# Moving the maximum of x, the normalising and the opening's order in a one-core attention and FP4 feed-forward kernel

## What is computed

```python
def fp4_quant_dequant(x):
    scale = max(max(abs(block)) / 6.0, 1e-12)
    idx = searchsorted(_MID, abs(block / scale))
    return _GRID[idx] * sign(block) * scale

x = x + attention(layernorm(x), ctx)
xn = layernorm(x)
h = silu(fp4_linear(xn, w_gate)) * fp4_linear(xn, w_up)   # 256 -> 704
x = x + fp4_linear(h, w_down)                             # 704 -> 256
```

## Time and profile before

| | |
|---|---|
| runs | 468.27, 468.79, 470.64 us (median 468.79) |
| the profiled execution | 469.22 us, of which span 467.4 us |
| busy in the span | PE 443.4 (95%), PEld 296.6, DVE 431.9 (92%), ACT 408.8 (87%), POOL 251.1 (54%) |
| granted TensorE clock, mean | 0.989 |
| chain that ended last | PE 40%, DVE 33%, issue 12%, DMA 6%, ACT 5% |

### The profile page before, as it was taken

The page is one execution under the profiler, slowest core; times in us unless marked ns, Lnnn a source line. Parts: engine busy times, 40 slices in busy tenths (PEclk is TensorE's granted clock), DMA queues, the critical chain, the costliest instruction groups (busy, mean ns, idle before and its releaser), DMA issues.

```text
span 467.4 us, 10007 instructions
## 1 busy us (share of the span) xinstructions
PE 443.4 (95%) x3388; PEld 296.6 (63%) x3388; DVE 431.9 (92%) x766; ACT 408.8 (87%) x710; POOL 251.1 (54%) x346
## 2 busy tenths in 40 slices
PE   4999998888699999999999999999999999999996
PEld 4987887734256666666666666666666666666675
DVE  3699979759999999999999999999999999999893
ACT  3369979779989999999999999999999999987694
POOL 4056872555566555566655566666666665433330
PEclk9999999999889999999999999999999999999999
DMA  7999911342267666666666666676656676655562
GB/s 242 338 349 350 356 34 35 80 111 60 64 120 127 141 140 141 139 137 131 131 130 131 137 139 147 133 141 131 142 131 139 140 124 135 120 114 122 121 136 78
DMA packets 162003, 67.95 MB, mean 145 GB/s; under 512 B 126368, under 2 KB 161696, under 8 KB 161952
## 3 DMA queue, kind: packets, MB, share of 16 engines
q1 hardware_dynamic: 161952, 67.31, 61.9%
HBM read 27.38 MB, written 9.18 MB: 78 GB/s over the span
## 4 chain that ended last, share of the span: by engine, by line
PE 40%; DVE 33%; issue 12%; DMA 6%; ACT 5%; SPq 2%; POOL 1%; DVEq 0%; ACTq 0%; POOLq 0%
PE ps L1056 7%; PE ps L1058 7%; PE ps L1057 7%; PE ps L1084 7%; DVE hb L1362 6%; DVE y_h L1473 6%; DVE bm L1479 4%; PE ps L1087 4%; DVE ctx_sb L1367 3%; DVE bm L1503 2%; PE ps L908 2%; PE ps L885 2%; DVE bm L1498 2%; PE ps L895 2%; DMA xs<-in_x_dram 2%
## 5 line engine op out<-in xcount | busy, mean ns | idle before, releaser
L1056 PE MATMUL ps<-guT_hi,a_xT 128*128 128x512 f16 (+1 forms) x384 | 140.5, 366 | 9.0 <-DVE hb L1362 5.5
L1057 PE MATMUL ps<-guT_lo,a_xT 128*128 128x512 f16 (+1 forms) x384 | 140.5, 366 | 0.0
L1058 PE MATMUL ps<-guT_hi,a_xT 128*128 128x512 f16 (+1 forms) x384 | 140.4, 366 | 0.0
L1084 PE MATMUL ps<-dT_hi,hqT 128*128 128x256 f16 x704 | 124.5, 273 | 0.9 <-ACT hqT L728 0.5
L545 POOL TENSOR_TENSOR ctx_sb<-w_q_lo,sl 128x704 f16<-128x704 f16 x60 | 90.1, 1520 | 4.1 <-DVE ctx_sb L1430 4.1
L1087 PE MATMUL ps<-dT_lo,hqT 128*128 128x256 f16 x384 | 87.4, 273 | 0.0
L1084 PEld LDWEIGHTS ps<-dT_hi,hqT 128*128 128x128 f16 x704 | 68.9, 98 | 11.0 <-issue 0.9
L561 POOL TENSOR_TENSOR sl<-bm,sh 128x240 f16<-128x240 f32 (+2 forms) x33 | 31.3, 949 | 78.4 <-DVE y_h L1473 73.9
L703 ACT ACTIVATE w_raw<-ps,inv_gu 128x704 f32<-128x704 f32 x64 | 53.8, 840 | 18.7 <-PE ps L1058 18.5
L628 POOL TENSOR_TENSOR xs<-xs,w_raw 128x512 f32<-128x512 f32 x30 | 36.9, 1229 | 61.8 <-DVE ctx_sb L1367 58.6
L1056 PEld LDWEIGHTS ps<-guT_hi,a_xT 128*128 128x128 f16 x384 | 38.0, 99 | 44.9 <-DMA a_xT<-ctx_sb 8.4
(11 more groups left out here) (189 smaller groups left out, 807.5 us busy)
## 6 DMA issues: line engine op xcount, KB each, us to landing
xs<-in_x_dram SPq DMA_DIRECT2D x16, 512.0 KB, 8.7
ctx_sb<-in_ctx_dram SPq DMA_DIRECT2D x16, 512.0 KB, 8.2
out_dram<-a_xT SPq DMA_DIRECT2D x64, 128.0 KB, 2.1
w_raw<-a_scratch SPq DMA_DIRECT2D x60, 128.5 KB, 2.7
hqT<-ctx_sb SPq DMA_TRANSPOSE x62, 3.8
w_raw<-in_L_ffn_w_down_dram SPq DMA_DIRECT2D x1, 704.0 KB, 8.0
w_raw<-in_L_ffn_w_gate_dram SPq DMA_DIRECT2D x1, 640.0 KB, 5.2
w_raw<-in_L_ffn_w_up_dram SPq DMA_DIRECT2D x1, 640.0 KB, 6.3
```

Of the source, the lines that this page charges most:

```text
L1056: pe.matmul(dst, xt[:, c, :], guT[0][:, c, n0:n1], start=(c == 0), stop=False)
L1057: pe.matmul(dst, xt[:, c, :], guT[1][:, c, n0:n1], start=False, stop=False)
L1058: last = pe.matmul(dst, xt[:, KC + c, :], guT[0][:, c, n0:n1], start=False, stop=(c == KC - 1))
L1084: last = pe.matmul(dst, hqT[:, j % 4, c, :], dT_hi[:, c, :], start=(c == 0 and not preset(j)), stop=(c == DCH - 1))
```

## The change

In a steady step two calls move: VectorE takes `largest_x(st + 3)` directly behind `inverses(st)`, ahead of `products_x`, and ScalarE calls `normalise_x(st + 3)` ahead of `silu(2 * st)` from step 2 on. The opening's loops are written out: ScalarE takes Silu(0) ahead of the normalising of pair 2 and Silu(1) ahead of that of pair 3, and the copies of weights later; POOL takes its additions ahead of the statistics and behind other events; VectorE takes the first two `gate_up` between parts of x(1) and x(2). TensorE gets fillers after pair 0 (7), before pair 2 (5) and after it (12), and its last weight transposes move from pair 1 to pair 2. In the drain `turn_last(0)` goes ahead of `down(61)` and `turn_last(1)` directly behind it, and ScalarE's last residual goes behind the first two copies of transposed h. The diff, cut (POOL's, ScalarE's and VectorE's functions that are called keep their bodies; `stats` and `attend` are POOL's two blocks made into functions):

```diff
@@ POOL
+            stats(1)
+            low_scales_first(1)
+            pool.wait_ge(s["x1_done"], 2)
+            pool.wait_ge(s["x4_steps"], K_XQ)
+            attend(2)
+            pool.wait_ge(s["yx_done"], 2)
+            attend(3)
+            low_scales(-1)
+            stats(2)
+            pool.wait_ge(s["x4_steps"], 2 * K_XQ)
+            attend(4)
+            stats(3)
+            low_scales(0)
+            pool.wait_ge(s["h_steps"], 2)
+            attend(5)
+            for st in range(1, END):
...
-                    elif st == 1:
-                        pool.wait_ge(s["x4_steps"], K_XQ * (st + 1) + 2)
                     else:
-                        need(pool, s["yx_done"], n - 2)
+                        pool.wait_ge(s["yx_done"], 4)
+                    attend(st + 5)
@@ ScalarE
             split_first(1)
-            for st in range(-2, END):
+            normalise_x(1)
+            evacuate_weights(act, range(GU_FILLS, GU_FILLS + 1))
+            square_x(2)
+            scale_high(-1)
+            split_x(1)
+            silu(0)
+            normalise_x(2)
+            square_x(3)
+            silu(1)
+            scale_high(0)
+            split_x(2)
+            normalise_x(3)
+            square_x(4)
+            for st in range(1, END):
                 j, n = st - 1, st + 2
-                if st < 0:
-                    if st == -1:
-                        scale_high(st)
-                        split_x(n)
-                    normalise_x(st + 3)
-                    square_x(st + 4)
-                    if st == -2:
-                        evacuate_weights(act, range(GU_FILLS, GU_FILLS + 1))
-                elif st == 0:
-                    silu(0)
-                    normalise_x(st + 3)
-                    square_x(st + 4)
-                    scale_high(st)
-                    silu(1)
-                    split_x(n)
-                    evacuate_weights(act, range(GU_FILLS + 1, GU_FILLS + 2))
-                elif st < NP:
+                if st < NP:
                     residuals(2 * st - 8)
                     square_x(st + 4)
                     scale_high(st)
                     residuals(2 * st - 7)
+                    if st >= 2:
+                        normalise_x(st + 3)
                     silu(2 * st)
                     preset_x(2 * st - 6)
-                    if st == 1:
-                        evacuate_weights(act, range(GU_FILLS + 2, GU_FILLS + 3))
-                    if st == 2:
-                        evacuate_weights(act, range(GU_FILLS + 4, len(FILLS)))
-                    normalise_x(st + 3)
+                    if st <= 2:
+                        evacuate_weights(act, range(GU_FILLS + 2 * st - 1, GU_FILLS + 2 * st))
+                    if st < 2:
+                        normalise_x(st + 3)
                     if st == NP - 1:
                         split_h(j)
                         preset_x(2 * st - 5)
                     silu(2 * st + 1)
+                    if st == 2:
+                        evacuate_weights(act, range(GU_FILLS + 4, len(FILLS)))
                     if st < NP - 1:
                         preset_x(2 * st - 5)
                         split_h(j)
                     split_x(n)
                     if st == 1:
-                        evacuate_weights(act, range(GU_FILLS + 3, GU_FILLS + 4))
+                        evacuate_weights(act, range(GU_FILLS + 2, GU_FILLS + 3))
...
                     residual(2 * NP - 4)
-                    residual(2 * NP - 3)
                     keep_turned(0)
                     keep_turned(1)
+                    residual(2 * NP - 3)
                     keep_turned(2)
                     keep_turned(4)
@@ TensorE
-                if final:
-                    if j % 2 == 0:
-                        out_ready(pe, 2 * NP - 5)
-                        turn_last(0)
-                elif preset(j):
+                if preset(j):
...
-                        if c:
-                            turn_last(1)
...
+                if n == NP + 2:
+                    out_ready(pe, 2 * NP - 5)
+                    turn_last(0)
                 if tile_ok(2 * n - 7):
                     down(2 * n - 7)
+                if n == NP + 2:
+                    turn_last(1)
                 if n == NP:
                     open_down(2 * NP - 4)
                 if pair_ok(n):
+                    if n == 2:
+                        pe.wait_ge(s["w_ev"], GU_FILLS + 2)
+                        filler(5, 7)
                     gate_and_up(2 * n)
-                    if n == 1:
+                    if n == 2:
                         transpose_weights(GU_FILLS + 3)
                     gate_and_up(2 * n + 1)
-                if n < 2:
-                    transpose_weights(GU_FILLS + 2 + 2 * n)
+                if n == 0:
+                    pe.wait_ge(s["w_ev"], GU_FILLS + 1)
+                    filler(7, 6)
+                    transpose_weights(GU_FILLS + 2)
+                if n == 2:
+                    pe.wait_ge(s["w_ev"], GU_FILLS + 3)
+                    filler(12, 6)
+                    transpose_weights(GU_FILLS + 4)
@@ VectorE
-            for st in range(-1, END):
+            scales(-1)
+            inverses(-1)
+            dve.wait_ge(sc, 2 * (-1 - SC0) + 2)
+            scaling_x(1)
+            offset_x(1)
+            grid_x(1)
+            products_x(1)
+            gate_up(0)
+            largest_x(2)
+            scales(0)
+            inverses(0)
+            dve.wait_ge(sc, 2 * (0 - SC0) + 2)
+            scaling_x(2)
+            gate_up(1)
+            largest_h(0)
+            offset_x(2)
+            grid_x(2)
+            products_x(2)
+            largest_x(3)
+            scales(1)
+            inverses(1)
+            dve.wait_ge(sc, 2 * (1 - SC0) + 2)
+            scaling_h(0)
+            scaling_x(3)
+            largest_x(4)
+            for st in range(2, END):
                 j, p, xa, xb = st - 1, st - 2, st + 1, st + 2
-                if st == 0:
-                    offset_x(xa)
-                    grid_x(xa)
-                    products_x(xa)
-                    largest_x(xb)
                 if pair_ok(j) and st < NP:
                     gate_up(2 * j)
-                    if st == 1:
-                        largest_x(3)
                     gate_up(2 * j + 1)
                     largest_h(j)
                 if st < NP:
@@ -1582,16 +1616,17 @@
                     scales(st)
                     if pair_ok(p):
                         grid_h(p)
-                    if st >= 1 and pair_ok(xa):
+                    if pair_ok(xa):
                         offset_x(xa)
                     if pair_ok(p) and st < NP - 1:
                         high_h(p)
-                    if st >= 1 and pair_ok(xa):
+                    if pair_ok(xa):
                         grid_x(xa)
                     if tile_ok(2 * st - 7) and added(2 * st - 7):
                         residual(2 * st - 7)
                     inverses(st)
-                    if st >= 1 and pair_ok(xa):
+                    largest_x(st + 3)
+                    if pair_ok(xa):
                         products_x(xa)
                     if scaled(st):
                         dve.wait_ge(sc, 2 * (st - SC0) + 2)
@@ -1602,8 +1637,6 @@
                         turned_product(p, 0, 1).then_inc(s["z_lo"], 1)
                     if pair_ok(xb):
                         scaling_x(xb)
-                    if st >= 1:
-                        largest_x(st + 3)
```

More of the change, by code:

```diff
@@ L585, in _, with stats, attend @@
             low_scales_first(0)
-            for st in range(-3, END):
+            def stats(n):
+                pool.wait_ge(s["sq_done"], n + 1)
+                need(pool, s["xn_ready"], n - 1)
+                pool.tensor_scalar(s_ve[:, n % 2], s_sq[:, n % 2], 1.0 / D, LN_EPS, ALU.mult, ALU.add).then_inc(s["pool_st"], 1)
+                pool.wait_ge(s["pool_st"], K_R * n + 1)
+                pool.tensor_tensor(s_r[:, n % 2], s_ve[:, n % 2], neg_half[:, 0:2], ALU.pow).then_inc(s["pool_st"], 1)
+                pool.wait_ge(s["pool_st"], K_R * n + 2)
+                pool.tensor_tensor(s_nmr[:, n % 2], s_nm[:, n % 2], s_r[:, n % 2], ALU.mult).then_inc(s["pool_st"], 1)
+            def attend(n):
+                pool.wait_ge(attn_loaded[n % 2], 32 * (n // 2))
+                need(pool, s["pool_st"], K_R * (n - 1))
+                x1 = xs[:, 2 * n:2 * n + 2, :]
+                pool.tensor_tensor(x1, x1, attn[:, n % 2, :, 0:D], ALU.add)
+                pool.tensor_tensor(s_nm[:, n % 2], neg_mean[:, 2 * n:2 * n + 2], attn[:, n % 2, :, D], ALU.add
+                                   ).then_inc(s["x1_done"], 1)
+            stats(1)
[14 more added lines that the diff above has]
+            for st in range(1, END):
                 if st == NP:
@@ L598, in _ @@
                         last_low_scales(t)
-                if st == -1:
[L600 to L609, removed]
```

(31 more changed lines are left out.)

1 line of the change is left out of this document (removed).

## The result

The changed kernel takes **476.7 us** (median of 8 runs, 475.89 to 478.94) against 468.87 (8 runs, 468.27 to 470.64) of the kernel before: ratio 1.0172, 95% interval 1.0152 to 1.0192. It is slower by 1.7%, as forecast (475.2, range 471 to 478).

The account below looks back on a forecast made before the run. It took the loop from one y_h to the next (VectorE, ScalarE's split and residual, TensorE) as the bound; 469.22 + 8.0 steady - 0.8 opening - 0.75 drain = 475.7, less 0.4: 475.2 us, range 471 to 478.

Parts of the forecast that it names:

- The steady steps: Steps 5 to 27: odd steps lengthen by 0.49 us and even ones by 0.18, +8.0 us over 12 pairs.
- Both covers: Steady steps: VectorE would wait for ScalarE's normalising in odd steps (+0.49 us) and for the split of h in even (+0.18).
- The opening: Before the steady steps: -0.3 us from the new order and -0.5 from the clock, sum -0.8.
- 12 pairs of steps: Steady stretch: the moves' cost was counted over odd steps 5 to 27, +0.67 us per pair, +8.0 us.
- My walk: Opening: followed the earlier gate_up(1) through pair 2, fillers and copies to the split of h(1); gain -0.3 us.
- The clock's -0.5: Opening: with fillers in TensorE's 3.74 us gap, full clock ends pair 3 earlier and removes a 0.50 us VectorE wait.
- upper bound of +2.5: Opening: the loss if the clock falls again in spite of the fillers, +2.5 us.
- The drain: Last pair: transposes ahead of down(61) remove TensorE's 0.55 us idle and half a residual; -0.75 us, between 0 and -1.0.
- The lock decides: Rival, steady steps: normalising and split are ready, the lock's 0.24 us per odd step is gained; 465.1 us, chance 0.09.
- Only the split is late: Rival, steady steps: only the split's wait costs, +0.12 us a pair, +1.4, cancelled by opening and drain; 468.7, chance 0.07.
- The clock falls: Rival, opening: TensorE drops to the lower clock again after a stall before pair 4; +2.5 us, 477.7, chance 0.08.
- The signs: Expected in the profile: odd-step normalising wait 0.5 to 0.7 us, even-step split wait 0.1 to 0.2, TensorE's wait about 0.4.

Follow-up runs that it names:

- E3: The kernel before with only VectorE's maximum of x moved behind the reciprocals, from step 2 on; ScalarE's order unchanged: 507.32 us, ratio 1.0823.
- E6: The changed kernel with the normalising also put ahead of ScalarE's second residual: 473.59 us, ratio 1.0088.
- E11: The changed kernel with the maximum of x behind the reciprocals in even steps only, back behind the scalings in odd ones: 470.22 us, ratio 1.0027.
- E12: The changed kernel with POOL's second low-half product of a step over half its columns from pair 4 on: 477.71 us, ratio 1.0195.
- E4: The kernel before with only ScalarE's normalising moved ahead of the first Silu, from step 2 on: 468.71 us, ratio 0.9996.
- E9: The kernel before with the drain's change alone: 467.99 us, ratio 0.9987.
- E2: The changed kernel with the two steady moves undone, keeping the new opening, fillers and drain: 466.65 us, ratio 0.9956.
- E10: E2 without its three fillers: 466.52 us, ratio 0.996.
- E1: The kernel before with only the two steady-step moves, from step 2 on; opening and drain as before: 478.19 us, ratio 1.0204.
- E5: The changed kernel with VectorE's small `scales` put ahead of the offset of h: 478.25 us, ratio 1.0177.
- E7: The changed kernel with both `scales` ahead of the offset and the normalising ahead of ScalarE's second residual: 474.31 us.
- E8: The kernel before with POOL's two low products of h put behind its statistics, beside VectorE's two-input operations: 488.45 us, measured once.

## Why the prediction was right, point by point

**The steady steps: right in mechanism, 0.8 small in size.** Both covers went, one by one as worked out. Odd steps came to 11.59 for 11.53, even ones to 11.38 for 11.36; the odd step's excess is in the two products behind the maximum, 225.99 - 225.32 = 0.67 instead of the 0.61 of the earlier trace rows, because the first no longer takes 0.36. Over twelve pairs the forecast was 8.0, measured 8.82. That the normalising sets the odd step is shown by E3 (1.1 us later, 1.1 us longer) and E6 (0.36 earlier, 0.36 shorter); that the split sets the even one by E11 and E12.

**The opening: the net near, its terms off, and that they cancelled is luck.** gate_up(1) came 3.14 us earlier (forecast 3.46), y_h of pair 0 and TensorE's pair 2 2.5 earlier (2.9). I forecast -0.8 for the whole and the profiled stretch to E of pair 3 gave -0.49, but as the difference of two larger terms. With the old steps that stretch takes 53.05, 51.94 and 52.51 with the old order (before, E4, E9; mean 52.5) and 50.85 and 50.59 with the new one (E2, E10; 50.7): the order is worth **-1.8**. With the changed steps it takes 53.63 with the old order (E1) and 51.79 to 52.56 with the new one (the changed kernel, E5, E6, E7, E12; mean 52.2): the steady moves cost **+1.1 to +1.5** here already, since they begin in step 2 (the maximum waits 0.44 at 121.01). The step that failed is "12 pairs of steps" from step 5 on: I costed the moves only where the step has its final form.

My walk gave the order -0.3. It was right in kind: the splits of h(0) and h(1), which start 0.04 behind y_h with the old order, start 1.1 and 0.9 to 1.9 behind it in all kernels with the new one, and that is where the gain goes. But with the old steps it took back too much (E2, E10). The clock's -0.5 rests on one execution: the 0.50 that VectorE waits at 139.75 stands in the trace of the kernel before, where the clock is 0.50 in 125 to 130 and the step takes 11.78; E9, with the same opening and the same gap of 3.74 us, has 0.71 there, no such wait and 11.19. With runs of one order 1.1 apart, no term here is better known than by some 0.5. One slip beside: the opening's upper bound of +2.5 put in for -0.8 gives 478.5, not the 477.5 of my numbers.

**The drain: right** where nothing hides it: -0.85 in E9's stage, -0.75 forecast. In the changed kernel's own profiled execution one slow DMA covered it.

**The sum.** E1's +9.5 and E2's -2.1 make 7.4; measured 7.8.

**The rivals.** *The lock decides* fell because the normalising is ready at E + 8.66, not + 8.0; E8 shows that the lock is no fiction. By the exclusive lock of the Trainium skill's page "SBUF — State Buffer" (who interferes with whom) alone the change should gain; E8 agrees with its rule, 1.67 against 0.88, and the order of the kernel decided otherwise. *Only the split is late* fell with the waits for L743. *The clock falls* did not happen: it is 1.00 in every 5 us from 110 to 150. The Trainium skill's page "TensorE: Matmul & The Clock Gate" (HAM oscillation) has the clock go back in waits between bursts. E10 agrees, with 2.40 us of idle time ahead of pair 2 and 0.73 behind it, and shows no price in its median.

**The signs.** L1519 waits 0.46 in every odd step (forecast 0.5 to 0.7); the even step's wait is 0.17 (0.1 to 0.2), seen as 1.71 for 1.54, since the table of waits does not list it; TensorE's wait at the opening matmul grew from 3.7 to 7.1 in 100 us, by 0.4 a step to 0.8; my "grown to about 0.4 a step" fits the growth only, since 3.7 in nine steps was 0.4 already; the 0.60 of the product is gone.

**The better version.** E2, and E10 with it, beats both kernels, the kernel before by 0.4%: 466.65 and 466.52 against its 468.7 and 468.4 beside them. Keep opening and drain, leave the steady steps as they were.

## What to carry to other kernels

An operation that seems to stand in the wrong place may be the cover of a wait on either side of it: before moving it, work out when its own input is ready, and what the next operation in its old slot would then wait for. When VectorE and ScalarE feed each other in a loop, 0.25 us saved on one is lost if the hand-over then comes 0.7 us early for the other. And a move made in every step has its price from the first step on that has it: count it in the opening too.

## What the runs showed of the hardware that I had not expected

- **POOL's smallest operations stretch most.** In the changed kernel the three statistics of 128x2 took 0.86, 1.42 and 0.56 us (231.76 to 234.76) beside VectorE's 16-bit operations with two SBUF inputs. In E8, where they fall beside VectorE's `gate_up`, which has one of its inputs in PSUM, they take 0.19, 0.70 and 0.19. Over the kernel the three come to 78.5 us instead of 35.5, which is more than POOL's 287.2 against 251.1; its other small operation, L600 (L629 before), fell from 12.5 to 5.9. Nothing waits for it here, but in even steps it is close: the last one ends at 234.76 and the normalising, which needs it, starts at 234.84.
- **A dependence costs VectorE about 0.1 us.** L1432 starts 0.92 behind the L1175 that it depends on, where an independent operation follows after 0.81 (232.49 - 231.68); behind the reduction L1495 a dependent operation starts after 1.65 (E5), an independent one after 1.54 (E11). A small independent operation between two dependent ones is partly free.
- **A fallen clock need not show in the time.** In 115 to 120 of E10 the clock is 0.73 and TensorE's busy column says 5.00 of 5, and still E10's stretch to E of pair 3 (50.59) is no longer than E2's (50.85).
